# Attention scores of four heads on four 32-row strips of TensorE, and the mask on VectorE

## The reference

```python
q = split_heads(x @ w_q)                            # 20 heads of 32
k, v = split_heads(text @ w_k), split_heads(text @ w_v)
out_text = softmax(q @ k.T / sqrt(32)) @ v
k_ip, v_ip = split_heads(ip @ w_k_ip), split_heads(ip @ w_v_ip)
out_ip = softmax(q @ k_ip.T / sqrt(32) + mask_ip) @ v_ip   # mask_ip: 0 or -10000, by token and image key
out = (out_text + out_ip) @ w_out + b_out + x
```

## Time and profile before

| | us |
|---|---|
| median of 3 runs | 904.82 (904.64 to 905.26) |
| the profiled execution | 905.81 |
| its span, first to last instruction | 904.0 |
| busy: PE / PEld | 882.5 / 753.8 |
| busy: DVE / ACT / POOL | 726.6 / 603.5 / 540.0 |
| a group, from its first score matmul to the next one's (480.84 to 531.31) | 50.5 |

### The profile page before, as it was taken

The page is one execution under the profiler, slowest core; times in us unless marked ns, Lnnn a source line. Parts: engine busy times, 40 slices in busy tenths (PEclk is TensorE's granted clock), DMA queues, the critical chain, the costliest instruction groups (busy, mean ns, idle before and its releaser), DMA issues.

```text
span 904.0 us, 13890 instructions
## 1 busy us (share of the span) xinstructions
PE 882.5 (98%) x4685; PEld 753.8 (83%) x4685; DVE 726.6 (80%) x1006; ACT 603.5 (67%) x986; POOL 540.0 (60%) x431
## 2 busy tenths in 40 slices
PE   7999999999999999999999999999999999999968
PEld 6889888888888888888888888888888888888846
DVE  6959579797888879797888879697888879797772
ACT  7556385876768485866767585867767584857550
POOL 5349669293755649293846648393847657392731
PEclk9999999999999999999999999999999999999978
DMA  9743322103030303003030303012030303010101
GB/s 318 271 162 117 96 69 86 44 1 131 1 124 1 131 0 102 21 13 118 0 123 0 131 0 122 2 33 98 0 123 0 131 0 116 0 59 1 47 12 59
DMA packets 34059, 64.63 MB, mean 71 GB/s; under 512 B 4464, under 2 KB 6512, under 8 KB 33904
## 3 DMA queue, kind: packets, MB, share of 16 engines
q1 hardware_dynamic: 33888, 62.97, 20.6%
q10 hardware_dynamic: 144, 1.31, 0.3%
HBM read 40.34 MB, written 23.59 MB: 71 GB/s over the span
## 4 chain that ended last, share of the span: by engine, by line
PE 82%; DVE 3%; ACT 1%; POOL 1%; issue 0%; DVEq 0%
PE bank L95 23%; PE bank L97 23%; PE bank L96 22%; PE bank L995 7%; PE bank L1004 4%; PE bank L1005 4%; DVE o_raw L905 1%; DVE pT_lo L898 1%; ACT oT_hi L820 0%; ACT pv_part L816 0%; POOL prob L185 0%; DVE total L226 0%; POOL prob L179 0%; DVE res L912 0%; ACT pT_hi L811 0%
## 5 line engine op out<-in xcount | busy, mean ns | idle before, releaser
L765 POOL TENSOR_TENSOR oT_lo<-o_raw,oT_hi 128x512 fp32r<-128x512 f32 x80 | 103.2, 1290 | 241.5 <-ACT oT_hi L820 241.5
L179 POOL TENSOR_TENSOR prob<-prob,top 128x1120 f32<-128x1120 f32 x126 | 178.8, 1448 | 0.0
L185 POOL TENSOR_TENSOR prob<-prob,inv 128x1120 f32<-128x1120 f32 x126 | 173.9, 1412 | 5.1 <-DVE inv L228 5.1
L95 PE MATMUL bank<-xT_hi,wq_hi 128*128 128x512 f32 x400 | 163.3, 408 | 0.0
L95 PE MATMUL bank<-oT_hi,wo_hi 128*128 128x512 f32 x400 | 156.7, 392 | 0.4 <-DVE res L912 0.4
L97 PE MATMUL bank<-xT_hi,wq_lo 128*128 128x512 f32 x400 | 156.8, 392 | 0.0
L96 PE MATMUL bank<-oT_lo,wo_hi 128*128 128x512 f32 x400 | 156.5, 391 | 0.0
L97 PE MATMUL bank<-oT_hi,wo_lo 128*128 128x512 f32 x400 | 156.5, 391 | 0.0
L96 PE MATMUL bank<-xT_lo,wq_hi 128*128 128x512 f32 x400 | 155.8, 389 | 0.0
L905 DVE TENSOR_TENSOR o_raw<-bank,pv_part 64x512 f32<-64x512 f32 x160 | 110.1, 688 | 47.2 <-ACT pv_part L816 44.8
L215 ACT ACTIVATE prob<-prob 128x1280 f32<-128x1280 f32 x64 | 81.6, 1277 | 78.6 <-POOL prob L179 78.5
(11 more groups left out here) (110 smaller groups left out, 1787.0 us busy)
## 6 DMA issues: line engine op xcount, KB each, us to landing
xin<-in_xT SPq DMA_DIRECT2D x16, 1280.0 KB, 6.8
outT<-res SPq DMA_DIRECT2D x80, 256.0 KB, 6.7
w_raw<-in_L_xattn_w_k SPq DMA_DIRECT2D x8, 320.0 KB, 5.6
w_raw<-in_L_xattn_w_k_ip SPq DMA_DIRECT2D x8, 320.0 KB, 5.7
w_raw<-in_L_xattn_w_v_ip SPq DMA_DIRECT2D x8, 320.0 KB, 3.1
w_raw<-in_L_xattn_w_v SPq DMA_DIRECT2D x8, 320.0 KB, 3.3
v_raw<-v_scratch SPq DMA_DIRECT2D x14, 140.0 KB
prob<-in_textT SPq DMA_DIRECT2D x8, 224.0 KB, 4.8
```

The costliest lines, as they stand in the source:

```text
L95: nc.tensor.matmul(dst, a_hi, b_hi, start=first, stop=False)
L179: ins = eng.tensor_tensor(s, s, top[:, t, n, :].unsqueeze(2).broadcast_to([P, HEADS, k1 - k0]), ALU.subtract)
L185: ins = eng.tensor_tensor(s, s, inv[:, t, n, :].unsqueeze(2).broadcast_to([P, HEADS, k1 - k0]), ALU.mult)
L765: nc.gpsimd.tensor_tensor(oT_lo[:, m, :], o_raw[:, m % 2, :], oT_hi[:, m, :].bitcast(F32), ALU.subtract).then_inc(oT_lo_done, 1)
```

## The change

The scores of a head are computed from that head's own 32 partitions: `qT[32 rows, 128 tokens]` is the weight, the head's 64 keys are the moving operand, and each of the four heads of a block writes to a bank of its own. The zero blocks of the keys, and the memsets that make them, are gone; `k_parts` holds 64 high and 64 low columns for each block. A group's scores are now 240 matmuls of 64 columns in three units of 5, 8 and 7 steps of (tile, block); units 0 and 2 use banks 0 to 3 and unit 1 banks 4 to 7. A unit is copied by four ACT instructions, one for each bank (12 in a group), in an order that frees banks 6 and 7 first.

The waits follow the banks: unit 0 waits for the last `pT_lo` of the group before, unit 1 for its last `add_pv`, unit 2 for unit 0's copies; out tiles 0 and 1 wait for the copies that free their banks.

The mask moves from POOL to DVE: `maxima` adds it in place ahead of its two reductions, and POOL's `add_mask` is gone. Building the keys is one ACT and one DVE instruction of 128 x 320.

```diff
         def k_hi_part(act, b, raw=None):
...
-            for j in range(HPT):
-                nc.scalar.activation(k_head(k_hi, j), raw[j * DH:(j + 1) * DH], ACT.Copy).then_inc(k_hi_built, 1)
+            nc.scalar.activation(k_parts[:, :, 0, :], raw, ACT.Copy).then_inc(k_hi_built, 1)
 
         def k_lo_part(dve, b, raw=None):
             raw = k_raw[:] if raw is None else raw
-            for j in range(HPT):
-                dve.wait_ge(k_hi_built, HPT * b + j + 1)
-                nc.vector.tensor_tensor(k_head(k_lo, j), raw[j * DH:(j + 1) * DH], k_head(k_hi, j).bitcast(F32), ALU.subtract).then_inc(k_built, 1)
+            dve.wait_ge(k_hi_built, b + 1)
+            nc.vector.tensor_tensor(k_parts[:, :, 1, :], raw, k_parts[:, :, 0, :].bitcast(F32), ALU.subtract).then_inc(k_built, 1)
...
+        SCORE_STEPS = ((0, KD), (KD, KD + 8), (KD + 8, GT * KD))
+        SCORE_COPIES = [(0, j) for j in range(HPT)] + [(1, j) for j in (2, 3, 0, 1)] + [(2, j) for j in (3, 0, 1, 2)]
+        UNITS = len(SCORE_COPIES)
...
         def units_for_tile(t):
-            return -(-(t + 1) * SW // 512)
+            return HPT * min(u + 1 for u, steps in enumerate(SCORE_STEPS) if steps[1] >= (t + 1) * KD)
...
-        def score_unit(pe, g, n, b, new_batch):
-            if n < 2:
-                wait(pe, score_copied, UNITS * g)
-            elif n < 4:
-                wait(pe, pT_lo_done, PAIRS * g)
+        def score_bank(u, j):
+            return bank[(0, 4, 0)[u] + j]
+
+        def score_unit(pe, g, u, b, new_batch):
+
+            if u == 0:
+                wait(pe, pT_lo_done, PAIRS * g)
+                if new_batch:
+                    pe.wait_ge(k_built, b + 1)
+            elif u == 1:
+                wait(pe, pv_added, PAIRS * g)
             else:
-                pe.wait_ge(score_copied, UNITS * g + n - 3)
-            if n == 0 and new_batch:
-                pe.wait_ge(k_built, HPT * (b + 1))
-            for half in range(2):
-                t, m = divmod(2 * n + half, KD)
+                pe.wait_ge(score_copied, UNITS * g + HPT)
+            first, last = SCORE_STEPS[u]
+            for step in range(first, last):
+                t, m = divmod(step, KD)
                 if t == 0:
                     pe.wait_ge(q_lo_done, KD * g + m + 1)
                 q_cols = slice(t * P, (t + 1) * P)
-                keys = [k[:, m, :, :].rearrange("p j k -> p (j k)") for k in (k_hi, k_lo)]
-                ins = three(s_bank[n % 4][:, half * CW:(half + 1) * CW], qT_hi[:, m, q_cols], qT_lo[:, m, q_cols], *keys, True, True)
+                cols = slice((step - first) * KEYS, (step - first + 1) * KEYS)
+                for n, (q, part) in enumerate(((qT_hi, 0), (qT_hi, 1), (qT_lo, 0))):
+                    for j in range(HPT):
+                        rows = slice(j * DH, (j + 1) * DH)
+                        ins = nc.tensor.matmul(score_bank(u, j)[:, cols], q[rows, m, q_cols], k_parts[rows, m, part, :], start=n == 0, stop=n == 2)
             ins.then_inc(score_ready, 1)
...
         def maxima(dve, g, t):
+            dve.wait_ge(score_copied, UNITS * g + units_for_tile(t))
+            text, ip = (tile(t)[:, :, k0:k1] for k0, k1 in SPANS)
+            m = mask[:, GT * g + t, :].unsqueeze(1).broadcast_to([P, HEADS, NIP])
+            nc.vector.tensor_tensor(ip, ip, m, ALU.add).then_inc(mask_added, 1)
+            nc.vector.tensor_reduce(top[:, t, 0, :], text, AX.X, ALU.max)
             dve.wait_ge(mask_added, GT * g + t + 1)
-            for n, (k0, k1) in enumerate(SPANS):
-                ins = nc.vector.tensor_reduce(top[:, t, n, :], tile(t)[:, :, k0:k1], AX.X, ALU.max)
-            ins.then_inc(max_done, 1)
+            nc.vector.tensor_reduce(top[:, t, 1, :], ip, AX.X, ALU.max).then_inc(max_done, 1)
...
                     if m >= 2:
                         pe.wait_ge(out_done, KD * g + m - 1)
                     elif more:
-                        pe.wait_ge(q_lo_done, KD * (g + 2))
+                        pe.wait_ge(score_copied, UNITS * (g + 1) + HPT + m + 1)
```

More of the change, by code:

```diff
@@ L83, in attention_kernel @@
         q_ready, q_hi_done, q_lo_done = sem("q_ready"), sem("q_hi_done"), sem("q_lo_done")
-        k_zeroed, k_raw_loaded, k_hi_built, k_built = (sem(n) for n in ("k_zeroed", "k_raw_loaded", "k_hi_built", "k_built"))
+        k_raw_loaded, k_hi_built, k_built = (sem(n) for n in ("k_raw_loaded", "k_hi_built", "k_built"))
         l_bank = bank[6:8]
@@ L201, in score_unit, with copy_scores @@
                 q_cols = slice(t * P, (t + 1) * P)
-                keys = [k[:, m, :, :].rearrange("p j k -> p (j k)") for k in (k_hi, k_lo)]
-                ins = three(s_bank[n % 4][:, half * CW:(half + 1) * CW], qT_hi[:, m, q_cols], qT_lo[:, m, q_cols], *keys, True, True)
-            ins.then_inc(score_ready, 1)
-        def copy_scores(act, g, u):
-            act.wait_ge(score_ready, UNITS * g + u + 1)
-            nc.scalar.activation(prob[:, u * 512:(u + 1) * 512], s_bank[u % 4][:], ACT.Copy).then_inc(score_copied, 1)
+                cols = slice((step - first) * KEYS, (step - first + 1) * KEYS)
[3 more added lines that the diff above has]
+                        ins = nc.tensor.matmul(score_bank(u, j)[:, cols], q[rows, m, q_cols], k_parts[rows, m, part, :], start=n == 0, stop=n == 2)
+            ins.then_inc(score_ready, 1)
+        def copy_scores(act, g, n):
+            u, j = SCORE_COPIES[n]
+            act.wait_ge(score_ready, len(SCORE_STEPS) * g + u + 1)
+            first, last = SCORE_STEPS[u]
+            dst = prob[:].rearrange("p (s j k) -> p s j k", j=HPT, k=KEYS)[:, first:last, j, :]
+            src = score_bank(u, j)[:, 0:(last - first) * KEYS].rearrange("p (s k) -> p s k", k=KEYS)
+            nc.scalar.activation(dst, src, ACT.Copy).then_inc(score_copied, 1)
         def exponentials(act, g, t, shared):
@@ L228, in sums @@
             nc.vector.reciprocal(inv[:, t, :, :], total[:, t, :, :]).then_inc(inv_done, 1)
[L230 to L234, removed]
         def sub_max(pool, g, t, count):
@@ L396, in _ @@
                         lo_chunk(c)
-                    for t in range(3):
-                        add_mask(pool, 0, t)
                     sub_max(pool, 0, 0, 1)
-                    add_mask(pool, 0, 3)
                     sub_max(pool, 0, 1, 1)
@@ L643, in text_values @@
                             if k == 0 and n % 2 == 0:
-                                pe.wait_ge(score_copied, UNITS if n == 0 else UNITS - 2)
+                                pe.wait_ge(score_copied, UNITS if n == 0 else UNITS - HPT + 1)
                             for i, at, c0, c1 in v_pieces(n):
@@ L682, in _ @@
                             ins.then_inc(k_ipT_ready, 1)
-                    for n in range(UNITS):
-                        score_unit(pe, 0, n, 0, True)
+                    for u in range(len(SCORE_STEPS)):
+                        score_unit(pe, 0, u, 0, True)
                     for k in range(KC):
                         if k == 0:
-                            pe.wait_ge(q_lo_done, KD)
+                            pe.wait_ge(score_copied, HPT + 2)
                         ip_tokens("v_ip", k, V_IP_BANKS, value_w_used, v_ip_ready)
@@ L845, in softmax @@
                         copy_scores(act, g, n)
-                        if n == 1:
+                        if n == HPT - 1:
                             oT_part(g - 1, KD - 1)
@@ L1021, in scores @@
                 def scores(g, b, new_batch, more):
-                    for n in range(UNITS):
-                        score_unit(pe, g, n, b, new_batch)
+                    for u in range(len(SCORE_STEPS)):
+                        score_unit(pe, g, u, b, new_batch)
                     for m in range(KD):
```

22 lines of the change are left out of this document (5 added, 17 removed).

## The result

The changed kernel takes 1037.38 us (median of 4 runs, 1034.6 to 1039.77), the kernel before 904.8: a ratio of 1.146, 95% interval 1.143 to 1.149. It is slower by 133 us, where 80 were forecast; the sign held, and the time lies inside the range of 890 to 1080, but 52 us above the value and above the 945 to 1020 that the forecast gave its own case.

What follows compares the result with a forecast made beforehand. PE, POOL and DVE run abreast in the out tiles, DVE only 0.6 us ahead of PE. Lateness 14 x 3.9 = 55, last group about 2, clock 14 x 1.7 = 24: +81 on 904.8, about 985 us, range 890 to 1080.

Steps and rivals of the forecast that it cites:

- its own case: Whole kernel: DVE late by 3 to 6 us a group, pair at 0.033 us or less; 945 to 1020, chance 0.60.
- DVE 0.6 us ahead of PE, so any delay stops PE: Out tiles: delaying DVE's maxima by over 0.6 us stops PE ahead of out tile 2, whatever the scores cost.
- The pair at 0.0275 us: Score stage: four weight loads run side by side, each at its 0.11 us, so the scores take 6.6 us.
- the rivals at 0.06: Score stage: load-matmul pairs limited by issue, scores 14.4 us, about 1078 us; chance 0.14 including 0.035 to 0.06.
- loads in turn: Score stage: weight loads run one after another, scores 26.4 us, +22 a group, about 1240 us; chance 0.11.
- The schedule of DVE: Softmax beside the out tiles: step times from the group's first score matmul (T), ending with out tile 2 at T+18.0.
- The whole lateness put on the mask: DVE's maxima: masks of 0.25 us plus waits for POOL's instructions make out tile 2 begin 3.9 us later.
- The clock at 1.7 a group, behind the wait at the out tiles: Behind PE's idle ahead of out tile 2: clock falls to 0.50 for two stretches, costing 1.7 us a group.
- The sum, 3.9 + 1.7 = 5.6 a group: Groups 1 to 14: out tile 2 begins 3.9 us later, plus 1.7 us for the fallen clock.
- The 0.3 us a group that the scores were to win: Score stage on PE: out tiles begin at T+7.0 instead of T+7.3, T being the group's first score matmul.
- Group 0 at nothing, the last group at 2: Ends of the span: group 0's softmax is covered by setup work, nothing; last group, without x parts, about 2 us.
- Keys, memsets, waits of out tiles 0 and 1 at nothing: Key building, setup memsets on POOL, and copy waits of the first two out tiles: each costs or gains nothing.

Runs made afterwards that it cites:

- e2: The kernel before with only the mask moved from POOL to DVE, scores unchanged on 128 rows: 962.4 us.
- e6: The changed kernel with the mask back on POOL, PE's loop over one group, and up to 256 key columns streamed per score matmul: 955.5 us.
- e10: The changed kernel, mask on DVE and loop of two groups kept, with up to 256 key columns streamed per score matmul: 1035.4 us.
- e5: The changed kernel with the mask back on POOL and PE's loop over one group instead of two: 982.1 us.
- e9: The changed kernel with mask on POOL, one-group loop, up to 256 columns per score matmul, and two orders changed on DVE and POOL: 913.8 us.
- e3: The changed kernel with PE's loop over one group instead of two: 1007.3 us.
- e4: The changed kernel with PE's loop written out, without a jump: 1007.8 us.
- e8: The changed kernel with the mask on POOL, PE's loop over one group, and up to 128 key columns streamed per score matmul: 957.0 us.

## Why the prediction was right, and where it was short

- **DVE 0.6 us ahead of PE, so any delay stops PE.** Right, and the main cause: DVE's addition ends a wait ahead of out tile 2 in all of groups 1 to 14, in the changed kernel as in e2, e6 and e10. Undoing the scores' part of the clock pays 27 us where DVE has been relieved of the mask (e5 to e6) and nothing where it has not (e10); the last wait goes with the orders of DVE and POOL (e9).
- **The pair at 0.0275 us.** Right: 0.113 for four, 0.028, while the clock is full. It is one load's time for four, and the rivals at 0.06 and with loads in turn are out. Four loads of one set and four of the next, in the changed kernel:

```profile
488.08 0.20 PEld L209 LDWEIGHTS bank<-k_parts,qT_hi 32*128 32x128 f32 x4
488.19 0.20 PEld L209 LDWEIGHTS bank<-k_parts,qT_lo 32*128 32x128 f32 x4
```

Four take 0.20 us, hardly more than the 0.19 of one, and the next four begin 0.11 later: they run side by side. The Trainium skill (TensorEngine Tiling (Array Packing), Key Properties) says that different tiles can load and multiply in parallel; the trace agrees. The Trainium skill (TensorEngine Tiling (Array Packing), Instruction Overhead) warns against tiling a dimension that is already small; the trace agrees here too, the set takes 0.113 us with 64 columns as with 128.
- **The schedule of DVE.** With the score clock held (e10), forecast against measured, from T: unit 2's copies 9.5 and 9.3; maxima of tile 0 5.5 and 5.4, tile 1 9.45 and 9.2, tile 2 11.3 and 13.0, tile 3 17.25 and 18.0; out tile 0 added 17.95 and 18.7; out tile 2 begun 18.0 and 18.8. The step that misses is tile 2: POOL's subtraction began at 495.59, 0.14 before the mask, and held it for 2.12 us; the prediction had the mask go first. Where the waits would sit was wrong (not in tiles 1 and 3), their sum nearly right.
- **The whole lateness put on the mask.** Too simple. The mask alone brings out tile 2 to T+16.2 (e2), the new units alone to T+16.2 (e6), both to T+18.8.
- **The clock at 1.7 a group, behind the wait at the out tiles.** Its size was right for the mask alone (e2: 3.41 us at half clock), its price was not: 0.4 us there, because a second wait for DVE goes with it. In the changed kernel the clock falls elsewhere: in the score stage. The prediction assumed full clock there and had no rival for it. Held there, it falls behind the wait instead (e10), for 6.83 us, of which some 2.5 are lost.
- **The sum, 3.9 + 1.7 = 5.6 a group.** Short, the first step that failed. e10 has the forecast's conditions, and its groups ahead of the first pause and behind the last take 57.7 to 58.0 us: 7.3 above the 50.5. The wait there is 4.4 us, and the clock is at half for 6.83, of which 1.8 lie inside the wait, so that some 2.5 are lost; 0.4 stays unexplained. The 0.3 us a group that the scores were to win did not come: out tiles begin at T+7.3 in e10 as in the kernel before.
- **The term that was missing: the jump back.** The prediction counted 240 pairs in place of 60 matmuls for PE's time and not for its instructions. Five pauses of 3.2 us, 16.2 us, and 27 with what follows them (e3, e4). Without them the time is 1007, inside the forecast's 945 to 1020.
- **Group 0 at nothing, the last group at 2.** Measured 4.5 with the setup and 3.2.
- **Keys, memsets, waits of out tiles 0 and 1 at nothing.** No wait in the trace of after contradicts it; none of them was tried alone.

Together: the groups of the changed kernel lose 14 x (8.6 - 5.6) = 42 us more than forecast, 16 of it in the pauses, 11 in the groups behind them, and 15 because a group without a pause takes 57.1 us and not 56.1; the ends add 6. These 48 are the difference between the forecast's +81 and the +128.5 of the profiled executions; the other 4 of the 52 lie between those and the medians. That 57.1 comes so near to 56.1 is luck in part: the forecast had a wait of 4.2 us and a fall behind it, and the nine groups without a pause ahead have the fall in front, 0.5 to 1.3 us of wait ahead of out tile 2 and 0.7 ahead of out tile 3.

## What to carry to other kernels

Where three engines run abreast, ask of an edit which chain ends last at the next meeting point, and don't add delays that lie beside each other: here a slow clock and a late VectorE lay largely beside each other, and undoing the first alone gave nothing, since the longer wait brought a fall of its own. Count the instructions of a loop's body as well as their time: quadrupling the smallest matmuls can make every jump back a stall, which a shorter body or a written-out loop removes. And a matmul that is paced by its weight load gets no faster by streaming less: four heads side by side with 64 columns took 0.113 us, one load with 256 columns 0.12.

## What the hardware showed that was not expected

- The clock can fall while PE shows next to no idle: in the changed kernel it went to 0.50 in the midst of the score matmuls (4.35 us after the first one in the group shown, in a stage with PE busy for 9.55 of 9.66 us), with sets of four following each other every 0.113 us. With up to 128 or 256 columns in the same matmuls, at nearly the same pace, it stayed at 1.0 there (e6, e8).
- At half clock the same sets took 0.213 us, so this stage, paced by loads, slows by 1.9 times with the clock.
- A return to the head of PE's loop cost 2.96 to 3.51 us with bodies of 1,800 and 2,160 loads and matmuls, nothing with 900 and 1,080, and nothing where the loop was written out (e4).
